# Third layer of a four-layer image kernel: powers taken from the unscaled symmetric matrix with a row scaling of each square, no transposition of the scaled matrix, and the last sum in token order

## Chip, cores and metric

The kernel runs on one core of one Trainium2 chip. The metric is the device time of one launch in microseconds (us). All tensors are float32 but for two small bfloat16 ones in the fourth layer.

## What is computed

The input is an image of 128 x 128 positions with 64 channels. Four layers follow one another, each as `x = x + layer(group_norm(x))`. The change is in the third layer alone. There, each of the 128 rows of the image is a graph of P = 128 nodes (tokens) with 64 features, and for every row the layer does this:

```python
def _build_A(pt, k):                       # k = 8
    x = pt - pt.mean(axis=-1, keepdims=True)
    x = x / (pt.std(axis=-1, ddof=1, keepdims=True) + 1e-06)
    corr = jnp.einsum('bnpd,bnqd->bnpq', x, x) / (D - 1 + 1e-06)
    ...                                    # mask: the 9 largest of each row of corr
    A = corr * mask
    A = 0.5 * (A + jnp.swapaxes(A, -1, -2))
    A = A + jnp.eye(P, dtype=A.dtype)
    deg = jnp.clip(A.sum(-1), 1e-06, None)
    dinv = deg ** (-0.5)
    return dinv[..., :, None] * A * dinv[..., None, :]
...
diff = alpha * (y - A y);  react = (A y) @ theta_w.T    # right side of an ODE, 8 Runge-Kutta steps of order 4
return relu(y_end)
```

The right side is linear in y, so eight steps are one polynomial of degree 32 in the matrix A = D^-1/2 M D^-1/2 (M symmetric 128 x 128, D its diagonal of degrees) and a 64 x 64 matrix that is the same for all rows. The kernel sums that polynomial in steps of A^4 and A^8 (Horner's rule).

## The kernel before, in words

The third layer is the function `layer2` (its name counts from 0), lines 1252 to 1667. It works on groups of ROWS = 4 rows, 32 groups. Every engine runs a loop of its own, written out by hand, over stages s = -1 to 33; in stage s the engines work on up to four groups at once, named by `stage(s)` (lines 1314 to 1317): `a` = s+1 (the next group is normed and transposed), `p` = s (the matrix M is prepared), `c` = s-1 (powers, and the first half of the polynomial), `r` = s-2 (the rest of the polynomial and the result). The order inside each loop is the order in which an engine issues; semaphores (`wait_ge`, `then_inc`) tie the engines together. PSUM, the memory that TensorE writes, has eight banks: B[0] squares, B[1] products with vectors, B[2] and B[3] (together `duo`) correlation, transpositions and the result, and four banks `quad`, one for each row of a group, which hold the running polynomial. SBUF tiles are slices of `nat` and `flat`.

One stage of TensorE, in its order, with the lines:

- L1574: transposes the normed tokens of `p`. L1528: `square(a1)`, which gives A^2 of `c`. L1540: one Horner step of `r` (two products of 128 x 128 by 128 x 128, accumulated in `quad`), after ACT has copied the last step's result out of `quad` (`keep_z`, L1362).
- L1547 and L1549, in `final(r, 0)`: the last sum. One transposition of the kept z for two rows, and two products whose stationary operand is z (64 columns) and whose moving operand is A^4, into the 64-partition halves of B[3], that is channel by token.
- L1591: sixteen instructions, y times A and y times A^2 for four rows. L1603: correlation of `p`. L1540, then L1528: A^4; L1611: transpositions; L1540; L1620: transposes the tokens of `a`.
- L1532: products with `theta`, 512 columns each, four calls, with `final(r, 1)`, L1637 and L1528 (A^8) between them. L1648: transposes the masked matrix of `p`. L1532: four more calls, and between them three Horner steps of `c` (L1540, `horner(c, 0, k)`) and L1662.
- L1662: transposes B = (scaled rows of M)/2 of `p` into B[3]; `b_ready` and `b_turned` stand around it. DVE then multiplies the rows of the transposed matrix with D^-1/2 again (L1516), which gives A (`a1`).

A call on a float32 operand is issued as two matmul instructions, a transposition as one.

The other engines, as far as they matter here:

- ACT copies every PSUM result that TensorE needs again: A^2 (L1389), A^4 (L1408), A^8 (L1422), the vectors (L1394, L1410, L1420), the correlation (L1399), the tokens (L1386, L1417), the Horner results (L1359, L1362), and takes two small square roots (L1425, L1428).
- DVE finishes a half group with three instructions (`finish`, L1439, L1442, L1444), finds the nine largest values of each row (L1455 to L1470), measures the next group (L1476, L1482), sums the degrees (L1487, L1491), takes reciprocals (L1496, L1501), scales rows (L1504), norms tokens (L1511), scales again (L1516) and sums the result for the next group norm (L1521, L1522).
- POOL adds the identity to the masked matrix (L1331), lays the finished group out for the fourth layer with four copies (L1343, L1344), and adds it into a sum (L1345). It does these in this order in each stage, and the copies wait for `x3_ready`.

## Time and profile before

| | us |
|---|---|
| three runs, median (lowest to highest) | 1161.11 (1156.29 to 1163.44) |
| the profiled execution, its own time | 1155.92 |
| its span, first to last instruction | 1154.1 |
| TensorE busy in the span | 1068.6 (93%) |
| VectorE (DVE) busy | 744.7 (65%) |
| ScalarE (ACT) busy | 522.6 (45%) |
| GpSimd (POOL) busy | 339.8 (29%) |

The profile is of one execution. PE is TensorE's matmuls, PEld its weight loads, which overlap them. A row of a timeline has the start, the duration from the first start to the last end of the instructions merged in it, the engine, the line, the operation, output and inputs by name with their shapes, and how many instructions are merged; in square brackets stands idle time just before, and what ended it. Matmuls are pipelined: the end of one overlaps the next, so what a block of them costs TensorE is the distance from its start to the start of the next block. A stage of the third layer recurs every 18.06 us; the stage looked at here begins at 706.56 us with L1574, and the next with the same instruction at 724.62.

### The profile page before, as it was taken

What the parts mean: (1) busy time and instruction counts of PE and PEld (TensorE: products, weight loads), DVE (VectorE), ACT (ScalarE), POOL (GpSimd) and SP (SyncE); (2) the same over time, 40 slices, a digit from 0 to 9 for tenths busy, and PEclk for the clock granted to TensorE, in tenths of its full rate; (3) what the DMA queues carried; (4) which work ended last, traced back from release to release, by engine and by line L of the source; (5) the groups of instructions that cost most, each with busy time, mean ns of one, the idle gap of its engine ahead of it and who ended that gap; (6) DMA issues with size and microseconds to landing.
All of it is one profiled execution on the core that took longest, in us unless ns stands there. A gap on an engine that the chain in (4) does not pass through costs nothing. (4 is left out here: it accounts for less than half of the span.)

```text
span 1154.1 us, 25407 instructions
## 1 busy us (share of the span) xinstructions
PE 1068.6 (93%) x9467; PEld 763.5 (66%) x9467; DVE 744.7 (65%) x3585; ACT 522.6 (45%) x1113; POOL 339.8 (29%) x476
## 2 busy tenths in 40 slices
PE   5887999999998799859999999999999999999788
PEld 3435888888886244437676776767777677776476
DVE  3675888888887332256767667676676766766245
ACT  2474777777776100134454444544445344453200
POOL 0142666666665100001212122121221212212211
PEclk8898999999999799869999999999999999999879
DMA  8000000000000000000000000000000000000012
GB/s 169 1 0 1 3 3 3 2 4 2 3 3 2 1 1 1 10 1 1 1 1 1 1 1 2 1 1 2 1 1 1 2 1 1 2 1 1 0 41 111
DMA packets 10461, 11.07 MB, mean 10 GB/s; under 512 B 3812, under 2 KB 8164, under 8 KB 10340
## 3 DMA queue, kind: packets, MB, share of 16 engines
q1 hardware_dynamic: 8964, 8.87, 2.9%
q8 instruction: 75, 1.23, 0.5%
q10 hardware_dynamic: 1376, 0.59, 0.3%
q14 instruction: 46, 0.38, 0.1%
HBM read 5.14 MB, written 4.23 MB: 8 GB/s over the span
## 5 line engine op out<-in xcount | busy, mean ns | idle before, releaser
L1532 PE MATMUL quad<-theta,nat 128*128 128x512 f32 x512 | 240.7, 593 | 0.0
L1331 POOL TENSOR_TENSOR nat<-nat,const 128x512 f32<-128x512 f32 x32 | 40.6, 1270 | 437.9 <-DVE nat L1470 437.9
L712 POOL TENSOR_TENSOR nat<-nat,arena 128x512 f32<-128x512 f32 x128 | 131.5, 1049 | 56.8 <-DVE arena L770 53.1
L1540 PEld LDWEIGHTS quad<-flat 128*128 128x128 f32 x768 | 104.9, 191 | 46.4 <-ACT flat L1362 25.0
L1532 PEld LDWEIGHTS quad<-theta,nat 128*128 128x128 f32 x512 | 87.5, 191 | 61.7 <-issue 61.7
L1540 PE MATMUL quad<-flat 128*128 128x128 f32 x768 | 124.1, 284 | 2.8 <-ACT flat L1362 1.7
L770 DVE CUSTOM_DVE_ANT_0 nat<-quad,arena 128x128 f32<-128x128 f32 x512 | 111.3, 283 | 2.0 <-PE quad L856 1.8
L1362 ACT ACTIVATE flat<-quad 128x256 f32<-128x256 f32 x192 | 73.3, 382 | 70.4 <-PE quad L1540 56.7
L729 ACT ACTIVATE nat<-bank 128x512 f32<-128x512 f32 x128 | 73.0, 597 | 65.8 <-PE bank L864 65.8
L1439 DVE SCALAR_TENSOR_TENSOR flat<-nat,c,duo 128x128 f32<-128x128 f32 x64 | 22.0, 344 | 102.6 <-PE duo L1549 102.6
L864 PE MATMUL bank<-const,nat 128*128 128x128 f32 x512 | 73.4, 276 | 8.0 <-ACT nat L729 8.0
L734 ACT ACTIVATE nat<-nat 128x512 f32<-128x512 f32 x128 | 77.2, 634 | 3.8 <-POOL nat L712 3.8
L1528 PE MATMUL bank<-nat 128*128 128x128 f32 x512 | 68.7, 278 | 0.3 <-DVE nat L1516 0.3
L864 PEld LDWEIGHTS bank<-const,nat 128*128 128x128 f32 x512 | 57.3, 141 | 15.9 <-ACT nat L729 15.6
L1528 PEld LDWEIGHTS bank<-nat 128*128 128x128 f32 x512 | 63.1, 194 | 0.8 <-DVE nat L1516 0.7
L1420 ACT ACTIVATE nat<-bank 128x512 f32<-128x512 f32 x32 | 19.1, 597 | 87.2 <-PE bank L1637 87.2
L1455 DVE MAX8 arena<-nat 128x8 f32<-128x128 f32 x128 | 27.9, 281 | 43.1 <-ACT nat L1399 43.1
L1487 DVE CUSTOM_DVE_ANT_0 nat<-nat,duo 128x128 f32<-128x128 f32 x128 | 29.2, 283 | 37.0 <-PE duo L1648 37.0
L770 DVE DVE_READ_ACCUMULATOR2_ANT arena<- 128x1 f32 x512 | 42.7, 83 | 0.0
L1344 POOL COPY img<-flat 64x256 f32<-64x256 f32 x64 | 39.6, 618 | 3.9
L1444 DVE SCALAR_TENSOR_TENSOR flat<-flat 128x128 f32<-128x128 f32 x64 | 38.3, 599 | 2.2
L840 PE MATMUL quad<-flat,w 64*128 64x256 f32 x256 | 37.2, 410 | 2.7 <-DVE arena L770 2.0
(393 smaller groups left out, 2236.7 us busy)
## 6 DMA issues: line engine op xcount, KB each, us to landing
out<-nat SPq DMA_DIRECT2D x16, 256.0 KB, 2.0
const<-in_constants ACTq DMA_DIRECT2D x1, 400.5 KB, 3.1
arena<-in_L_conv_Ws SPq DMA_DIRECT2D x1, 240.0 KB
flat<-arena SPq DMA_DIRECT2D x3, 32.0 KB, 4.4
nat<-in_x SPq DMA_DIRECT2D x4, 0.2 KB, 11.6
arena<-in_L_conv_Wq ACTq DMA_DIRECT2D x1, 32.0 KB, 6.2
arena<-in_L_conv_Wk ACTq DMA_DIRECT2D x1, 32.0 KB, 5.3
arena<-in_L_conv_Wv ACTq DMA_DIRECT2D x1, 32.0 KB, 5.0
```

The costliest lines, as they stand in the source:

```text
L712: pool.tensor_tensor(scored, scored, of_head(least[b], h).broadcast_to([128, ROWS, L]), ALU.subtract).then_inc(lowered, 1)
L729: act.activation(pT[r], m.bank[r % 2][:, :], ACT.Copy).then_inc(kept, 1)
L734: act.activation(t, t, ACT.Exp, scale=-1.0).then_inc(exps_done, 1)
L770: last = dve.tensor_tensor_reduce(prob[b][:, at(r, h)], m.quad[:, h, row(r)], m.bias[:, row(h)], -1.0, BIG, ALU.add, ALU.min, least[b][:, ...
L864: last = pe.transpose(m.bank[r % 2][:, row(h)], prob[g % 2][:, at(r, h)], ident)
L1331: pool.tensor_tensor(quarters(rem), quarters(rem), ident.unsqueeze(1).broadcast_to([128, ROWS, 128]), ALU.add).then_inc(diag_added, 1)
L1344: step(pool.tensor_copy(m.cols3[:, :, ROWS * r + e:ROWS * (r + 1):2].rearrange("p j t -> p t j"), source))
L1362: act.activation(kept, m.quad[:, HALF * half:HALF * (half + 1), place * C:(place + 2) * C], ACT.Copy).then_inc(z_ready[half], 1)
L1444: dve.scalar_tensor_tensor(out=x_of(g, half), in0=held[half], scalar=0.0, in1=x_of(g, half), op0=ALU.max, op1=ALU.add).then_inc(x3_ready[h ...
L1528: last = pe.matmul(B[0][:, col(n)], source[:, col(n)], source[:, col(n)], start=True, stop=True)
L1532: return pe.matmul(m.quad[:, n, :], vT[:, col(n)], m.theta[:, part, :], start=(part == 0), stop=False, skip_group_check=True)
L1540: last = pe.matmul(m.quad[:, row, place * C:(place + 2) * C], a8[g % 2][:, col(row)], zs[half][k % 2][:, n, :], start=False, stop=(k == 2) ...
```

## The change

The unscaled matrix M is used in place of A, with S = D^-1: the kernel keeps A1 = S M, and squares as (S M)^T times M = M S M. A square is then the symmetric "plain" matrix (`h2`, `h4`), and multiplying its rows with S gives the "scaled" one (`a2`, `a4`, `a8`). So:

- The transposition L1662 and the product L1516 behind it are gone, as are `b_ready` and `b_turned`. DVE makes `a1` with one scaling of the summed matrix (new L1530).
- A^2 and A^4 are copied out of PSUM by ACT (`h2`, new L1397; `h4`, new L1417) and then scaled, A^2 by DVE (new L1473, both inputs in SBUF) and A^4 by POOL (new L1331). A^8 is scaled by DVE straight out of PSUM (new L1513), and ACT's copy L1422 is gone.
- The tokens enter scaled by D^1/2, by POOL in place (new L1341, `yn_weighed`), and the result is scaled back with D^-1/2 by DVE (`weigh`, new L1451).
- The last sum is made in token order: `sum_up` (new L1579) has A^4 as the stationary operand (128 columns), 64 moving columns, and accumulates into `quad`; after `weigh`, two transpositions (new L1675) bring the group to channel order in B[3], and DVE finishes the whole group at once with two instructions (`finish`, new L1458, L1461), now near the end of its stage.
- On TensorE the correlation (L1603, now L1621) stands ahead of the products with A and A^2 (L1591, now L1630). ACT's order of the two copies (L1394, L1399) is as before.

TensorE, steady state, in the kernel before, at the end of a stage: the first two Horner steps of group `c`, with the transposition of B between them:

```order
L1540 MATMUL quad<-flat 128x128 [waits l2_z_ready_first,l2_a8_ready]
L1540 MATMUL quad<-flat 128x128
L1662 MATMUL duo<-const,nat 128x128 [waits l2_held_ready_last,l2_b_ready]
L1662 MATMUL duo<-const,nat 128x128 x3
L1540 MATMUL quad<-flat 128x128 [waits l2_z_ready_first]
```

The same place on TensorE in the changed kernel, up to the first instructions of the next stage:

```order
L1570 MATMUL quad<-flat 128x128 [waits l2_z_ready_first,l2_a8_ready]
L1570 MATMUL quad<-flat 128x128
L1570 MATMUL quad<-flat 128x128 [waits l2_z_ready_first]
L1570 MATMUL quad<-flat 128x128
L1562 MATMUL quad<-theta,nat 128x512
L1570 MATMUL quad<-flat 128x128 [waits l2_z_ready_first]
```

Between the two Horner steps nothing stands now. TensorE in the kernel before, at the start of a stage (turn of the normed tokens, `square`, Horner step, `final`, the products with A and A^2, the correlation):

```order
L1574 MATMUL duo<-const,nat 128x128 [waits l2_xs_ready]
L1574 MATMUL duo<-const,nat 128x128
L1528 MATMUL bank<-nat 128x128 [waits l2_a8_ready,l2_a1_ready]
L1528 MATMUL bank<-nat 128x128 x3
L1540 MATMUL quad<-flat 128x128 [waits l2_z_ready_last]
L1540 MATMUL quad<-flat 128x128
L1547 MATMUL duo<-const,flat 128x128 [waits l2_z_ready_first,l2_held_ready_last]
L1549 MATMUL duo<-flat 64x128 x2
L1591 MATMUL bank<-nat 64x128 [waits l2_v34_ready,l2_a2_ready]
L1591 MATMUL bank<-nat 64x128 x7
L1603 MATMUL duo<-nat 128x128 [waits l2_a1_ready,l2_held_ready_first,l2_xsT_ready]
L1603 MATMUL duo<-nat 128x128 x3
```

And the same place on TensorE in the changed kernel:

```order
L1604 MATMUL duo<-const,nat 128x128 [waits l2_xs_ready]
L1604 MATMUL duo<-const,nat 128x128
L1558 MATMUL bank<-nat 128x128 [waits l2_a8_ready,l2_a1_ready]
L1558 MATMUL bank<-nat 128x128 x3
L1570 MATMUL quad<-flat 128x128 [waits l2_z_ready_last]
L1570 MATMUL quad<-flat 128x128
L1579 MATMUL quad<-flat 128x64 [waits l2_z_ready_first]
L1579 MATMUL quad<-flat 128x64
L1621 MATMUL duo<-nat 128x128 [waits l2_held_ready,l2_xsT_ready]
L1621 MATMUL duo<-nat 128x128 x3
L1630 MATMUL bank<-nat 64x128 [waits l2_v34_ready,l2_a2_ready,l2_yn_weighed]
L1630 MATMUL bank<-nat 64x128 x7
```

`final`'s three calls became two with 64 moving columns, and the correlation moved ahead of the products that wait for `a2_ready`.

DVE in the kernel before, across the end of a stage: the norm of the tokens, the second scaling, the sums of the finished group, and then `finish` of the next group's first half ahead of the search:

```order
L1511 TENSOR_SCALAR nat<-nat,arena 128x64 x3
L1516 TENSOR_TENSOR nat<-duo,arena 128x512 [waits l2_b_turned]
L1521 BN_STATS stats<-flat 128x6 [waits l2_x3_ready_last,l2_x3_ready_first]
L1522 TENSOR_REDUCE rowsum<-flat 128x2
L1439 SCALAR_TENSOR_TENSOR flat<-nat,c,duo 128x128 [waits l2_final_made_first]
L1442 TENSOR_TENSOR flat<-flat,duo 128x128 [waits l2_held_ready_first]
L1444 SCALAR_TENSOR_TENSOR flat<-flat 128x128 [waits l2_held_ready_first]
L1455 MAX arena<-nat 128x8 [waits l2_cor_ready]
```

The same place on DVE in the changed kernel: `finish` of a whole group, its sums, then the scaling of A^2 and `weigh`:

```order
L1545 TENSOR_SCALAR nat<-nat,arena 128x64 x3
L1458 SCALAR_TENSOR_TENSOR flat<-nat,c,duo 128x256 [waits l2_final_made]
L1461 SCALAR_TENSOR_TENSOR flat<-flat 128x256 [waits l2_held_ready]
L1551 BN_STATS stats<-flat 128x6 [waits l2_x3_ready]
L1552 TENSOR_REDUCE rowsum<-flat 128x2
L1473 TENSOR_TENSOR nat<-nat,arena 128x512 [waits l2_v34_made,l2_h2_ready]
L1451 TENSOR_TENSOR flat<-quad,arena 128x128 [waits l2_final_made,l2_summed]
L1480 MAX arena<-nat 128x8 [waits l2_cor_ready]
```

In the kernel before, `finish` of the second half (again L1439, L1442, L1444) stood right behind the search (L1470), so the instruction that releases POOL's copies has moved from the middle of the stage to its end. POOL's order in a stage was L1331 (identity), copies, L1345; it is now the product for A^4 (new L1331), the identity (new L1337), the product on the tokens (new L1341), copies, sum. The core of the diff:

```diff
@@ gpsimd
+                if c is not None:
+                    pool.wait_ge(h4_ready, c + 1)
...
+                    pool.tensor_tensor(quarters(a4[c % 2]), quarters(h4), square_inv.unsqueeze(2).broadcast_to([128, ROWS, L]),
+                                       ALU.mult).then_inc(a4_ready, 1)
...
+                    pool.wait_ge(dsq_ready, p + 1)
+                    fresh = quarters(yn[p % 2])
+                    pool.tensor_tensor(fresh, fresh, dsq.unsqueeze(2).broadcast_to([128, ROWS, C]), ALU.mult).then_inc(yn_weighed, 1)
@@ scalar
-                    act.activation(a2, B[0][:, :], ACT.Copy).then_inc(a2_ready, 1)
+                    act.activation(h2, B[0][:, :], ACT.Copy, scale=0.5).then_inc(h2_ready, 1)
...
-                    act.activation(a4[c % 2], B[0][:, :], ACT.Copy).then_inc(a4_ready, 1)
+                    act.activation(h4, B[0][:, :], ACT.Copy).then_inc(h4_ready, 1)
...
-                    act.wait_ge(a8_made, c + 1)
-                    act.activation(a8[c % 2], B[0][:, :], ACT.Copy).then_inc(a8_ready, 1)
@@ vector
+            def weigh(g, half):
+                dve.wait_ge(summed, 2 * g + half + 1)
...
+                dve.tensor_tensor(weighed[half].rearrange("p (n x) -> p n x", n=HALF), m.quad[:, HALF * half:HALF * (half + 1), 0:C],
+                                  dinv[g % 4][:, HALF * half:HALF * (half + 1)].unsqueeze(2).broadcast_to([128, HALF, C]),
+                                  ALU.mult).then_inc(weighed_ready, 1)
+            def finish(g):
+                dve.wait_ge(final_made, g + 1)
+                dve.scalar_tensor_tensor(out=held, in0=yT[g % 4], scalar=m.c0[:, :], in1=B[3][:, 0:PAIR],
+                                         op0=ALU.mult, op1=ALU.add).then_inc(held_ready, 1)
+                dve.wait_ge(held_ready, g + 1)
+                dve.scalar_tensor_tensor(out=x_of(g), in0=held, scalar=0.0, in1=x_of(g),
+                                         op0=ALU.max, op1=ALU.add).then_inc(x3_ready, 1)
...
+                if c is not None:
+                    dve.wait_ge(h2_ready, c + 1)
...
+                    dve.tensor_tensor(quarters(a2), quarters(h2), by_degree(square_inv), ALU.mult).then_inc(a2_ready, 1)
...
+                    dve.tensor_tensor(quarters(a8[c % 2]), quarters(B[0][:, :]), by_degree(square_inv), ALU.mult).then_inc(a8_ready, 1)
...
-                    dve.wait_ge(b_turned, p + 1)
-                    dve.tensor_tensor(quarters(a1), quarters(B[3][:, :]), dinv.unsqueeze(2).broadcast_to([128, ROWS, L]),
-                                      ALU.mult).then_inc(a1_ready, 1)
                 if r is not None:
+                    finish(r)
@@ tensor
-            def square(source):
+            def square(scaled, plain):
                 for n in range(ROWS):
-                    last = pe.matmul(B[0][:, col(n)], source[:, col(n)], source[:, col(n)], start=True, stop=True)
+                    last = pe.matmul(B[0][:, col(n)], scaled[:, col(n)], plain[:, col(n)], start=True, stop=True)
...
-                pe.transpose(B[3][:, L:2 * L], zs[half][1][:, 0, :], ident)
-                for e in range(HALF):
-                    last = pe.matmul(B[3][e * C:(e + 1) * C, 0:L], zs[half][1][:, 1, e * C:(e + 1) * C], a4[g % 2][:, col(HALF * half + e)],
-                                     start=True, stop=True, skip_group_check=True)
+                for n in range(HALF):
+                    row = HALF * half + n
+                    last = pe.matmul(m.quad[:, row, 0:C], a4[g % 2][:, col(row)], zs[half][1][:, n, 0:C],
+                                     start=False, stop=True, skip_group_check=True)
+                last.then_inc(summed, 1)
...
+                    for half in range(2):
+                        last = pe.transpose(B[3][:, col(half)], weighed[half], ident)
+                    last.then_inc(final_made, 1)
...
-                    pe.wait_ge(b_ready, p + 1)
...
-                    for n in range(ROWS):
-                        last = pe.transpose(B[3][:, col(n)], cor[:, col(n)], ident)
-                    last.then_inc(b_turned, 1)
```

## Rows read from the trace of the kernel before

**Rows 1.** Busy time of the engines, third layer; the last columns are granted clock, DMA share, GB/s

```profile
525.00:1067.00 542.00, 540.97 (x3661) 389.76 (x3660) 375.01 (x1876) 247.29 (x598) 120.69 (x180) 1.00 0.01 1
```

**Rows 2.** Timeline of TensorE's matmuls, end of one stage and the next

```profile
703.62 0.61 PE L1540 MATMUL quad<-flat 128*128 128x128 f32 x4
704.10 0.66 PE L1662 MATMUL duo<-const,nat 128*128 128x128 f32 x4
704.71 0.71 PE L1540 MATMUL quad<-flat 128*128 128x128 f32 x4
...
706.56 0.38 PE L1574 MATMUL duo<-const,nat 128*128 128x128 f32 x2
706.78 1.06 PE L1528 MATMUL bank<-nat 128*128 128x128 f32 x8
707.67 0.61 PE L1540 MATMUL quad<-flat 128*128 128x128 f32 x4
708.12 0.27 PE L1547 MATMUL duo<-const,flat 128*128 128x128 f32 x1
...
708.59 1.04 PE L1591 MATMUL bank<-nat 128*64 128x128 f32 x16
709.58 0.71 PE L1603 MATMUL duo<-nat 64*128 64x128 f32 x8
710.22 0.71 PE L1540 MATMUL quad<-flat 128*128 128x128 f32 x4
...
714.49 0.27 PE L1547 MATMUL duo<-const,flat 128*128 128x128 f32 x1
...
715.06 1.16 PE L1637 MATMUL bank<-nat 128*128 128x128 f32 x8
...
718.66 0.60 PE L1648 MATMUL duo<-const,nat 128*128 128x128 f32 x4
```

**Rows 3.** Timeline of TensorE's matmuls, last stages of the layer

```profile
1081.13 0.61 PE L1540 MATMUL quad<-flat 128*128 128x128 f32 x4
1082.21 0.71 PE L1540 MATMUL quad<-flat 128*128 128x128 f32 x4 [0.47 <-ACT flat L1362]
```

**Rows 4.** Timeline of TensorE in the second layer, and clock of that stretch (columns as in rows 1)

```profile
415.81 1.94 PE L1232 MATMUL quad<-const,arena 1*128 1x1 f32 x16
417.69 0.64 PE L1169 MATMUL quad<-img,arena 64*64 64x512 f32 x1
...
415.50:417.70 2.20, 2.20 (x20) 1.87 (x19) 0.00 (x0) 0.00 (x0) 0.00 (x0) 1.00 0.00 0
```

**Rows 5.** Timeline of ACT in the same stage as rows 2

```profile
707.87 0.60 ACT L1389 ACTIVATE nat<-bank 128x512 f32<-128x512 f32 x1 [0.18 <-PE bank L1528]
...
709.68 0.60 ACT L1394 ACTIVATE nat<-bank 128x512 f32<-128x512 f32 x1 [0.94 <-PE bank L1591]
710.33 0.60 ACT L1399 ACTIVATE nat<-duo 128x512 f32<-128x512 f32 x1
```

**Rows 6.** Timeline of DVE in that stage

```profile
709.51 0.29 DVE L1444 SCALAR_TENSOR_TENSOR flat<-flat 128x128 f32<-128x128 f32 x1
710.96 0.87 DVE L1455 MAX8 arena<-nat 128x8 f32<-128x128 f32 x4 [1.16 <-ACT nat L1399]
...
715.00 0.69 DVE L1470 SCALAR_TENSOR_TENSOR nat<-nat 128x512 f32<-128x512 f32 x1
715.61 0.34 DVE L1439 SCALAR_TENSOR_TENSOR flat<-nat,c,duo 128x128 f32<-128x128 f32 x1
...
716.31 0.95 DVE L1444 SCALAR_TENSOR_TENSOR flat<-flat 128x128 f32<-128x128 f32 x1
...
719.30 0.29 DVE L1487 CUSTOM_DVE_ANT_0 nat<-nat,duo 128x128 f32<-128x128 f32 x1 [1.11 <-PE duo L1648]
...
720.26 0.21 DVE L1491 TENSOR_SCALAR arena<-arena 128x4 f32<-128x4 f32 x1
...
720.95 0.88 DVE L1504 TENSOR_SCALAR nat<-nat,arena 128x128 f32<-128x128 f32 x4
721.74 0.98 DVE L1511 TENSOR_SCALAR nat<-nat,arena 128x64 f32<-128x64 f32 x4
```

**Rows 7.** Timeline of POOL in that stage

```profile
715.84 1.27 POOL L1331 TENSOR_TENSOR nat<-nat,const 128x512 f32<-128x512 f32 x1 [13.18 <-DVE nat L1470]
717.42 0.39 POOL L1343 COPY img<-flat 64x256 f32<-64x256 f32 x1 [0.30 <-DVE flat L1444]
...
719.71 0.73 POOL L1345 TENSOR_TENSOR arena<-arena,flat 128x256 f32<-128x256 f32 x1
```

More of the change, by code:

```diff
@@ L1275, in layer2 @@
     yn = [t[:, k:k + PAIR] for t in (next(nat_tiles),) for k in (0, PAIR)]
-    cor, rem, a1, a2, v12T, v12n, v34T = (next(nat_tiles) for _ in range(7))
+    cor, rem, a1, h2, a2, h4, v12T, v12n, v34T = (next(nat_tiles) for _ in range(9))
     a4, a8 = ([next(flat_tiles) for _ in range(2)] for _ in range(2))
     zs = [[t[:, k:k + PAIR].rearrange("p (n x) -> p n x", n=HALF) for t in (next(flat_tiles),) for k in (0, PAIR)] for _ in range(2)]
-    held = [t[:, 0:L] for t in (next(flat_tiles), next(flat_tiles))]
+    held = next(flat_tiles)[:, 0:PAIR]
+    weighed = [t[:, k:k + L] for t in (next(flat_tiles),) for k in (0, L)]
     st = m.take(6 * ROWS)
     mv = m.take(2 * ROWS).rearrange("p (r s) -> p r s", s=2)
-    std, rstd, deg, dsq, dinv = (m.take(ROWS) for _ in range(5))
+    std, rstd, deg, dsq, square_inv = (m.take(ROWS) for _ in range(5))
+    dinv = [m.take(ROWS) for _ in range(4)]
     top = m.take(8 * ROWS)
@@ L1471, in _ @@
                 if r is not None:
-                    finish(r, 1)
+                    weigh(r, 1)
                 if a is not None:
@@ L1491, in _ @@
                     dve.tensor_scalar(deg, deg, 0.5, 1e-6, ALU.mult, ALU.max).then_inc(deg_ready, 1)
+                    dve.wait_ge(deg_ready, p + 1)
+                    if p > 0:
+                        dve.wait_ge(a4_ready, p)
+                    dve.reciprocal(square_inv, deg).then_inc(square_inv_ready, 1)
+                    dve.wait_ge(square_inv_ready, 2 * p + 1)
+                    if p > 0:
+                        dve.wait_ge(a2_made, p)
+                    for n in range(ROWS):
+                        last = dve.tensor_scalar(a1[:, col(n)], cor[:, col(n)], square_inv[:, n:n + 1], 0.5, ALU.mult, ALU.mult)
+                    last.then_inc(a1_ready, 1)
                 if a is not None:
@@ L1498, in _ @@
                     dve.wait_ge(dsq_ready, p + 1)
[L1499 to L1505 removed]
+                    dve.reciprocal(dinv[p % 4], dsq).then_inc(square_inv_ready, 1)
                 if a is not None:
@@ L1542, in horner, with sum_up @@
                 last.then_inc(horner_made[half], 1)
[L1544 removed]
+            def sum_up(g, half):
                 pe.wait_ge(z_ready[half], 4 * g + 4)
[L1547 to L1551 removed]
+                for n in range(HALF):
[3 more added lines that the diff above has]
+                last.then_inc(summed, 1)
             def kind_weights():
@@ L1579, in _ @@
                         pe.wait_ge(a8_ready, c)
-                    square(a1).then_inc(a2_made, 1)
+                    square(a1, cor).then_inc(a2_made, 1)
                 if r is not None:
                     horner(r, 1, 0)
-                    pe.wait_ge(held_ready[1], 2 * r)
-                    final(r, 0)
+                    sum_up(r, 0)
+                if p is not None:
+                    pe.wait_ge(xsT_ready, p + 1)
+                    if r is not None and r > 0:
+                        pe.wait_ge(held_ready, r)
+                    for t in range(HALF):
+                        for e in range(2):
+                            half = xsT[e * C:(e + 1) * C, col(t)]
+                            last = pe.matmul(B[2 + e][:, col(t)], half, half, start=True, stop=True)
+                    last.then_inc(cor_made, 1)
                 if c is not None:
+                    pe.wait_ge(yn_weighed, c + 1)
                     pe.wait_ge(a2_ready, c + 1)
@@ L1593, in _ @@
                     last.then_inc(v12_made, 1)
-                if p is not None:
-                    pe.wait_ge(xsT_ready, p + 1)
-                    if r is not None:
-                        pe.wait_ge(held_ready[0], 2 * r + 2)
-                    if c is not None:
-                        pe.wait_ge(a1_ready, c + 1)
-                    for t in range(HALF):
-                        for e in range(2):
-                            half = xsT[e * C:(e + 1) * C, col(t)]
-                            last = pe.matmul(B[2 + e][:, col(t)], half, half, start=True, stop=True)
-                    last.then_inc(cor_made, 1)
                 if r is not None:
@@ L1629, in _ @@
                 if r is not None:
-                    if p is not None:
-                        pe.wait_ge(cor_ready, p + 1)
-                    pe.wait_ge(held_ready[0], 2 * r + 2)
-                    final(r, 1)
+                    sum_up(r, 1)
                 if c is not None:
@@ L1656, in _ @@
                     horner(c, 0, 0)
-                if p is not None:
-                    pe.wait_ge(b_ready, p + 1)
-                    if r is not None:
-                        pe.wait_ge(held_ready[1], 2 * r + 2)
-                    for n in range(ROWS):
-                        last = pe.transpose(B[3][:, col(n)], cor[:, col(n)], ident)
-                    last.then_inc(b_turned, 1)
                 if c is not None:
```

88 lines of the change are left out of this document (44 added, 44 removed).

## The prediction

> **What bounds the kernel now.** I read busy time by stretch first, then TensorE's timeline over one stage, then those of ACT, DVE and POOL at the same times. In the third layer TensorE is busy 540.97 of 542.00 us at a granted clock of 1.00, its level of 2.4 GHz, and DVE, ACT and POOL 375, 247 and 121 us [rows 1]. So the layer costs what TensorE's stage costs, 18.06 us, unless another engine makes TensorE wait. In rows 2 the reader is to take distances between starts: 706.56 to 706.78 is 0.22 us for two transpositions, 706.78 to 707.67 is 0.89 for eight instructions of 128 columns, 0.111 each. "Busy" hides one thing: from 704.10 to 704.71 TensorE spends 0.61 on four transpositions (L1662) that take 0.44 at 0.111 each; it is waiting there.
>
> **The change part by part.** All offsets are from the start of a stage, 706.56.
>
> *L1662 goes, and returns nothing.* It stands between the Horner steps that start at 703.62 and 704.71, 1.09 apart [rows 2]. The second needs ACT's copy of the first's result. In the drain, where no L1662 stands between them, the same two start at 1081.13 and 1082.21, 1.08 apart, the second released by ACT L1362 [rows 3]. The transpositions lay inside that wait. What is late next is the copy itself, as before: gain 0.01, taken as 0.
>
> *The last sum.* `final` takes 0.47 (708.12 to 708.59) and 0.57 (714.49 to 715.06), 1.04 together [rows 2]. In its place come two calls of `sum_up` for each half, eight instructions in a stage, and two transpositions, 0.22 as L1574. No row has 64 moving columns behind a load of 128 at the full clock. From below: if moving columns set the pace, half of 0.111, 0.055. From above: sixteen instructions with one moving column and 128 loaded take 415.81 to 417.69, 0.117 each, at a clock of 1.00 [rows 4]. That row is nearer, since narrowing to one column did not make them faster than 128 columns: the load sets the pace. I take 0.11: 0.88 + 0.22 - 1.04 = +0.06 us a stage. With 0.055 it is 0.44 + 0.22 - 1.04 = -0.38. The Trainium skill ("TensorE: Matmul & The Clock Gate", section "Back-to-back issue gap") has about 60 cycles for a matmul of up to 64 columns, 0.025 us at 2.4 GHz; by it the sum would be 0.20 + 0.22 - 1.04 = -0.62. Its section on LDWEIGHTS has the number of loaded columns over 1.2 in ns, 107 ns here, which agrees with the 0.117 of rows 4 and not with its other figure.
>
> *The scaled A^2, a longer path into the sixteen instructions (L1630).* The square starts at +0.22; ACT began its copy at +1.31 and took 0.60 [rows 5], so `h2` is there at +1.91. DVE, idle then, starts the new product at +1.94. It is of L1470's kind and shape (two SBUF inputs, 128 x 512): 0.69 [rows 6], so `a2` would be there at +2.63 and L1630 start at +2.68. TensorE's cover, with the correlation (709.58 to 710.22, 0.64) moved ahead, is 0.22 + 0.89 + 0.45 + 0.44 + 0.64 = 2.64. Undisturbed, the wait is 0.04.
>
> *But POOL is at work then.* DVE's second L1444 takes 0.95 from 716.31, against 0.29 at 709.51 [rows 6]; both its inputs are in SBUF. POOL's L1331 runs from 715.84 to 717.11 [rows 7], and L1444 ends at 717.26: it stood until POOL was done, and ended 0.15 later. In the kernel before, POOL idles when a stage begins. Now its copies wait for `x3_ready` from the end of DVE's stage. Working that out: from L1648 to the next stage's start is 724.62 - 718.66 = 5.96, all TensorE's and unchanged. DVE starts the degree sums 0.64 after L1648 and L1491 0.96 later [rows 6]; then the reciprocal (0.20) and its result (0.21), four scalings 0.79 (720.95 to 721.74), three small ones 0.58, L1545 0.98, `finish` 0.48 and 0.43 (0.34 and 0.29 for 128 columns, and 0.13 for 128 more, which is what 512 against 128 columns cost L1470: 0.40 for 384), and 0.07 for two hand-overs: 0.64 + 0.96 + 0.41 + 0.79 + 0.58 + 0.98 + 0.98 = 5.34. POOL starts 0.16 after such an end (717.26 to 717.42), at 5.50, thus 0.46 before the stage ends. Its five instructions take 3.02 (717.42 to 720.44) [rows 7], so the last, L1353, runs from about +1.8 to +2.5. DVE's product comes at +1.94, in the midst of it, and stands until about +2.5 (from my steps, +2.48 to +2.56; I take 2.48). It then ends 0.15 + 0.40 later, at +3.03, and L1630 starts at +3.05: wait 0.41. Behind L1630 everything on TensorE shifts by it. Bounds: 0.04 where the product meets a gap, 0.6 where it meets L1353's start (0.73 to stand).
>
> *What is hidden.* ACT's correlation copy still stands behind its copy of L1630's result, so the search starts later: in the kernel before at +4.40 (710.96), now at 3.05 + 0.99 + 0.10 + 0.65 + 0.63 = +5.42 [rows 2, 5, 6]. `weigh` of the second half starts 4.65 later (710.96 to 715.61), takes about 0.29, and is there at +10.4. The theta product that waits for it stands 0.64 and 0.13 nearer to L1630 than before: 715.06 - 708.59 = 6.47, less 0.77, is 5.70, and 16 instructions of 0.111 are 1.8, so it comes at 3.05 + 7.5 = +10.55. So 0.15 of slack, the thinnest one. POOL's identity ends about +11.6, L1682 comes at +12.6. POOL's new product for A^4, 1.27 as L1331, ends about +7.6, the square that needs it comes at +9.75. ACT loses a copy of 0.60, DVE gets 0.69 for A^8 inside its wait for L1648 (1.11 idle in rows 6), and POOL's product on the tokens ends a stage ahead of its use. All these cost nothing; without that cover `weigh` would cost what it is late.
>
> *Sum.* L1630 starts at +3.05 instead of 2.03 + 0.64 = 2.67 with the correlation counted: +0.38. The second half: 0.44 + 0.22 - 0.57 = +0.09. Together +0.47 a stage, over 30 stages +14.1. At the ends: one stage without a correlation has 0.5 less cover; the last group has one more hop between DVE and TensorE, about 0.6; the first search starts some 0.4 later behind ACT. With +1.5 for these the sum is +15.6. Against the profiled execution's own 1155.92 (a span of 1154.1 and 1.8 around it) that is 1171.5. That execution lies 5.2 below the median of the three runs, so I put the sum on the mean of all four times, 1159.2: 1174.8.
>
> **The rivals.**
>
> *No clash on the port.* If POOL's phase is 0.3 later than I worked out, DVE's product slips in before L1353, or if 0.5 earlier, behind it. For it: my chain of 12 steps decides about 0.25 us. Against it: POOL is at work for 3.0 us around that time, and most shifts only change which instruction DVE meets. Per stage 0.04 + 0.09 = 0.13: 3.9 + 1.5, 1164.6. Chance 0.27.
>
> *Narrow matmuls at half price.* With the clash, L1630's start is fixed by `a2`, so only the second half gains: 0.38 + 0.22 + 0.22 - 0.57 = +0.25 a stage, 1168.2; without the clash -0.09 a stage, 1158. Rows 4 speak against. Chance 0.07.
>
> *Faster: L1662's time comes back.* If the second Horner step at 704.71 waited for L1662's own delay (it shares the queue with `b_ready`) and not for ACT's copy, 0.61 a stage goes: 0.47 - 0.61 = -0.14, 1156.5 with the clash, and -0.48 a stage, 1146.3, without. It decides from the point where two Horner steps can start less than 1.08 apart; rows 3 show they can't. With other gains that I don't see, chance 0.09.
>
> *The search is slowed by POOL.* POOL's product for A^4 runs from about +6.3 to +7.6, in the midst of DVE's search. If it blocked the search for up to 1.27, `weigh` would be up to 1.0 late for theta: up to 30 us more, 1195 for two thirds of that. No row has POOL and this search at one time. The search's instructions have one SBUF tensor each, unlike L1444. Chance 0.07. The Trainium skill ("SBUF — State Buffer", section "Who interferes with whom") says that a DVE instruction with at most one SBUF input, outside certain modes, does not contend with GpSimd; by it this rival costs nothing and the clash on A^2 stands.
>
> **How the numbers follow.** Forecast 0.50, no clash 0.27, half price 0.07, faster 0.09, slowed search 0.07. A measurement here can tell about 1% (11.6 us) from no change. The forecast's own range is 1168 to 1180 (a wait of 0.2 to 0.6). Slower by over 1% is above 1170.8: most of the forecast and the slowed search, 0.48. Within 1%: no clash, half price, the weak end of the forecast, half of the faster case: 0.44. Faster by over 1%: 0.08. The range runs from 1157 (the faster case with the clash) to 1184 (a full wait, put on the median of 1161.1).
>
> **What would show it.** Right: L1570 to L1570 at the end of a stage still 1.08 apart, now with idle time between; eight L1579 at 0.11 each; L1473 taking 1.1 instead of 0.69 and ending 0.15 + 0.40 after POOL's L1353; TensorE waiting about 0.4 before L1630 for DVE L1473; a stage of 18.5 us. Wrong: L1473 at 0.69 (no clash), L1579 at 0.06, Horner steps closer than 1.08, or waits of theta (L1562) for DVE L1451.

## The result, and the profile after

The changed kernel takes 1178.49 us (median of four runs, 1175.56 to 1180.79) against 1161.33 for the kernel before, measured beside it (four runs, 1156.29 to 1163.44). The ratio is 1.0156, its 95% interval 1.0124 to 1.0188: slower by 1.6%. The forecast was 1174.8, within 1157 to 1184. The profiled execution took 1175.56 with a span of 1173.7, so +19.6 in both against before. Offsets below count from a stage's start, the first transposition of normed tokens (L1574 before, L1604 after).

First the third layer by windows, the row that answers to [rows 1]: window and length, then busy us (and instructions) of TensorE, its loads, DVE, ACT and POOL, TensorE's clock, DMA share and GB/s.

```profile
525.00:1067.00 542.00, 514.38 (x3429) 383.54 (x3430) 376.45 (x1830) 211.71 (x553) 165.69 (x227) 1.00 0.00 1
```

At the same clock TensorE now idles 27.6 of 542 us, where it idled 1.0. ACT has lost 36 us of work, POOL gained 45. The view of waits, for TensorE from 540 to 1085, says before which line the idle time stands, and what ended it (us in all, times, longest):

```profile
PE quad L1570 <- ACT flat L1368: 14.2, 30, 0.5
PE bank L1630 <- issue: 14.0, 26, 0.5
```

Two waits share it. The first is the one in which L1662 used to stand and which cost time before, too. The second is new. It has no releaser in this view, so the lines that it could wait for have to be read. TensorE's timeline over one stage, 713.17 to 731.88, for [rows 2]:

```profile
710.24 0.61 PE L1570 MATMUL quad<-flat 128*128 128x128 f32 x4
711.32 0.71 PE L1570 MATMUL quad<-flat 128*128 128x128 f32 x4 [0.47 <-ACT flat L1368]
...
713.17 0.38 PE L1604 MATMUL duo<-const,nat 128*128 128x128 f32 x2
713.39 1.06 PE L1558 MATMUL bank<-nat 128*128 128x128 f32 x8
...
714.73 0.56 PE L1579 MATMUL quad<-flat 128*128 128x64 f32 x4
715.22 0.71 PE L1621 MATMUL duo<-nat 64*128 64x128 f32 x8
716.48 1.09 PE L1630 MATMUL bank<-nat 128*64 128x128 f32 x16 [0.54 <-issue]
...
723.99 1.88 PE L1562 MATMUL quad<-theta,nat 128*128 128x512 f32 x4
...
731.88 0.38 PE L1604 MATMUL duo<-const,nat 128*128 128x128 f32 x2
```

A stage takes 18.71 where it took 18.06. L1630 starts at +3.31. TensorE was free at 715.94 (its row less the 0.54 of idle time), at +2.77. DVE and POOL at the same time, for [rows 6] and [rows 7]:

```profile
715.12 1.26 DVE L1473 TENSOR_TENSOR nat<-nat,arena 128x512 f32<-128x512 f32 x1 [1.71 <-ACT nat L1397]
...
723.39 0.28 DVE L1451 TENSOR_TENSOR flat<-quad,arena 128x128 f32<-128x128 f32 x1
...
727.94 1.23 DVE L1530 TENSOR_SCALAR nat<-nat,arena 128x128 f32<-128x128 f32 x4
...
730.90 0.42 DVE L1461 SCALAR_TENSOR_TENSOR flat<-flat 128x256 f32<-128x256 f32 x1
```

```profile
715.10 0.72 POOL L1353 TENSOR_TENSOR arena<-arena,flat 128x256 f32<-128x256 f32 x1
719.82 1.04 POOL L1331 TENSOR_TENSOR flat<-nat,arena 128x512 f32<-128x512 f32 x1 [3.99 <-ACT nat L1417]
728.01 0.69 POOL L1341 TENSOR_TENSOR nat<-nat,arena 128x256 f32<-128x256 f32 x1 [3.13 <-ACT arena L1438]
731.49 0.39 POOL L1351 COPY img<-flat 64x256 f32<-64x256 f32 x1 [2.79 <-DVE flat L1461]
```

DVE's product is ready to start at +1.95, 0.02 after POOL's L1353 has started. POOL is done at 715.82, DVE at 716.38, 0.56 later, and TensorE starts at 716.48. So DVE stood until POOL was done, and then worked 0.56.

The profile also holds stages without the clash. In the one that starts at 695.03 DVE was the first, by 0.09:

```profile
695.03 0.38 PE L1604 MATMUL duo<-const,nat 128*128 128x128 f32 x2
...
697.77 1.09 PE L1630 MATMUL bank<-nat 128*64 128x128 f32 x16
```

```profile
696.98 0.69 DVE L1473 TENSOR_TENSOR nat<-nat,arena 128x512 f32<-128x512 f32 x1 [1.58 <-ACT nat L1397]
```

```profile
697.07 1.18 POOL L1353 TENSOR_TENSOR arena<-arena,flat 128x256 f32<-128x256 f32 x1
```

Here DVE took 0.69, POOL was the one that was held (1.18 instead of 0.72), L1630 came at +2.74 and the stage (to 713.17) took 18.14. The next stage fell into the clash. Another of these stages, which starts at 825.38, shows which of POOL's instructions matters:

```profile
827.32 0.69 DVE L1473 TENSOR_TENSOR nat<-nat,arena 128x512 f32<-128x512 f32 x1 [1.49 <-ACT nat L1397]
```

```profile
826.81 0.62 POOL L1352 COPY img<-flat 64x256 f32<-64x256 f32 x1
```

DVE started while POOL's copy still had 0.11 to go, and took its 0.69 all the same. So the copy did not hold it, where the sum, L1353, does.

Over the layer the 29 stages from 527.28 to 1067.40 take 540.1, where the same 29 took 523.6 before (526.02 to 1049.59): +16.5 of the 19.6. The rest is at the two ends: the first of these stages starts 1.3 later, the end of the layer is 1.0 longer (up to the first matmul behind it, at 1095.68 before and 1114.48 after), and 0.8 come behind that.

### The profile page after: what moved, and what is told of

Read it like the earlier page. It is cut to its first block and busy times, and to the rows that moved or that the text cites. A ratio compares the mean times of both kernels' runs of the same rounds, so it can differ in the third digit from the quotient of the medians.

```text
span 1173.7 us, 25304 instructions
## 1 busy us (share of the span) xinstructions
PE 1059.5 (90%) x9339; PEld 771.6 (66%) x9339; DVE 758.5 (65%) x3585; ACT 491.9 (42%) x1081; POOL 397.2 (34%) x540
## 5 line engine op out<-in xcount | busy, mean ns | idle before, releaser
L1562 PE MATMUL quad<-theta,nat 128*128 128x512 f32 x512 | 240.9, 593 | 0.0
L1562 PEld LDWEIGHTS quad<-theta,nat 128*128 128x128 f32 x512 | 87.4, 191 | 61.2 <-issue 61.2
L1331 POOL TENSOR_TENSOR flat<-nat,arena 128x512 f32<-128x512 f32 x32 | 33.3, 1041 | 135.6 <-ACT nat L1417 135.6
L1337 POOL TENSOR_TENSOR nat<-nat,const 128x512 f32<-128x512 f32 x32 | 40.6, 1269 | 102.6 <-DVE nat L1495 102.6
L1473 DVE TENSOR_TENSOR nat<-nat,arena 128x512 f32<-128x512 f32 x32 | 36.8, 1149 | 58.3 <-ACT nat L1397 58.3
L1351 POOL COPY img<-flat 64x256 f32<-64x256 f32 x64 | 25.4, 397 | 99.3 <-DVE flat L1461 97.3
L1341 POOL TENSOR_TENSOR nat<-nat,arena 128x256 f32<-128x256 f32 x32 | 21.8, 682 | 98.7 <-ACT arena L1438 98.7
L1630 PE MATMUL bank<-nat 128*64 128x128 f32 x512 | 35.9, 282 | 14.9 <-issue 14.6
```

The costliest lines, as they stand in the source:

```text
L1337: pool.tensor_tensor(quarters(rem), quarters(rem), ident.unsqueeze(1).broadcast_to([128, ROWS, 128]), ALU.add).then_inc(diag_added, 1)
L1473: dve.tensor_tensor(quarters(a2), quarters(h2), by_degree(square_inv), ALU.mult).then_inc(a2_ready, 1)
L1562: return pe.matmul(m.quad[:, n, :], vT[:, col(n)], m.theta[:, part, :], start=(part == 0), stop=False, skip_group_check=True)
L1630: last = pe.matmul(B[1][e * C:(e + 1) * C, col(n)], yn[c % 2][:, col(n, C)], power[:, col(n)], start=True, stop=True, skip_group_check=True)
```

## The experiments

The theory: L1473 stands behind POOL's L1353, 0.56 a stage, and nearly all of the loss is that. The rivals: TensorE's own order and the new last sum cost it; or the missing L1662 plays a part. Each ratio below is against the kernel before, run beside it.

**POOL's copies moved out of the way.** They and the sum (put together as `lay`) go behind the product for A^4, a stage later:

```diff
+                if r is not None and r > 0:
+                    if c is not None:
+                        pool.wait_ge(a4_ready, c + 1)
+                    lay(r - 1)
```

> The changed kernel, but POOL lays a group out and adds it to the sum one stage later, behind its product for A^4, so that it is idle when DVE scales A^2. Theory (port clash): DVE's L1473 takes 0.69 us instead of 1.26, TensorE stops waiting ahead of the products with A and A^2 (L1630), the stage goes from 18.70 to about 18.2 us, and the time from 1178 to about 1163. Rival (the wait is the extra hop over DVE itself, not the clash): L1473 shorter or not, stage and time stay within 3 us of the changed kernel.

Measured: 1162.63, ratio 1.0029 (1.0013 to 1.0044). TensorE's timeline, then DVE's:

```profile
710.07 0.38 PE L1606 MATMUL duo<-const,nat 128*128 128x128 f32 x2
...
728.21 0.38 PE L1606 MATMUL duo<-const,nat 128*128 128x128 f32 x2
```

```profile
712.01 0.69 DVE L1475 TENSOR_TENSOR nat<-nat,arena 128x512 f32<-128x512 f32 x1 [1.70 <-ACT nat L1399]
```

The product starts at +1.94, as in the changed kernel, takes 0.69, and the stage 18.14. All work is still there, only its time differs. The clash alone is 18.70 - 18.14 = 0.56 a stage. In the new place one of POOL's copies meets the last instruction of the search (L1497 here, two SBUF inputs, 128 x 512) with 0.37 to go, and that instruction takes 0.75 instead of 0.69: 0.06 beside a copy, against 0.57 beside the sum.

**The product read from PSUM.** DVE scales A^2 straight from TensorE's result; ACT's copy and the next square are ordered behind it.

```diff
-                    dve.wait_ge(h2_ready, c + 1)
+                    dve.wait_ge(a2_made, c + 1)
...
-                    dve.tensor_tensor(quarters(a2), quarters(h2), by_degree(square_inv), ALU.mult).then_inc(a2_ready, 1)
+                    dve.scalar_tensor_tensor(out=quarters(a2), in0=quarters(B[0][:, :]), scalar=0.5, in1=by_degree(square_inv),
+                                             op0=ALU.mult, op1=ALU.mult).then_inc(a2_ready, 1)
```

> The changed kernel, but DVE makes the scaled A^2 straight out of PSUM (one SBUF input), ahead of ACT's copy h2. Theory: an instruction with one SBUF input isn't held up by POOL, so it takes 0.69 us although POOL's copies run, a2 is there 1.2 us earlier, no wait ahead of the products with A and A^2, stage about 18.2 us, time about 1163. Rival (any DVE work beside POOL's is slowed): L1473's successor still takes 1.1 to 1.3 us; the time still falls, by less, since it starts 0.6 us earlier.

Measured: 1161.68, ratio 1.0022 (1.0007 to 1.0038), a stage of 18.09 (709.10 to 727.19). DVE:

```profile
710.41 0.69 DVE L1474 SCALAR_TENSOR_TENSOR nat<-bank,arena 128x512 f32<-128x512 f32 x1 [1.08 <-PE bank L1560]
```

In this stage it is mostly a copy that POOL works on beside it (L1352, 710.31 to 710.94), which would not have held the old product either. One stage, at the end of the layer, has the sum at work before DVE starts:

```profile
1071.89 0.69 DVE L1474 SCALAR_TENSOR_TENSOR nat<-bank,arena 128x512 f32<-128x512 f32 x1 [2.11 <-PE bank L1560]
```

```profile
1071.47 0.72 POOL L1353 TENSOR_TENSOR arena<-arena,flat 128x256 f32<-128x256 f32 x1
```

POOL's sum had 0.30 to go, and DVE took 0.69, where the product from SBUF, meeting the last 0.34 of the same sum, takes 0.89 (next experiment). The Trainium skill ("SBUF — State Buffer", section "Who interferes with whom") exempts DVE instructions with at most one SBUF input, outside certain modes; here the inputs are PSUM and a small SBUF one, and the trace agrees. The product is also ready 1.2 earlier, so the time of this run alone does not part the port from the hop over ACT; the experiment before it does.

**A shorter product on the tokens.** Only the first of 64 channels is scaled, the others are left unscaled, to see what sets POOL's phase:

```diff
-                    pool.tensor_tensor(fresh, fresh, dsq.unsqueeze(2).broadcast_to([128, ROWS, C]), ALU.mult).then_inc(yn_weighed, 1)
+                    pool.tensor_tensor(fresh[:, :, 0:1], fresh[:, :, 0:1], dsq.unsqueeze(2), ALU.mult).then_inc(yn_weighed, 1)
```

> The changed kernel with POOL's product on the tokens cut from 256 to 4 columns; the rest of the tokens stays unscaled, so that work is left out. Theory (phase of POOL's work): DVE's four scalings L1530 take 0.88 us instead of 1.23, DVE finishes the group 0.35 us earlier, POOL's sum ends 0.35 us earlier, L1473 takes about 0.9 instead of 1.26 us, stage about 18.35, time about 1168. Rival (L1473's length doesn't depend on POOL's phase): the same 18.70 and 1178.

Measured: 1168.79, ratio 1.0091 (1.0061 to 1.0121), a stage of 18.33 (715.67 to 734.00). DVE:

```profile
730.06 0.88 DVE L1530 TENSOR_SCALAR nat<-nat,arena 128x128 f32<-128x128 f32 x4
...
735.94 0.89 DVE L1473 TENSOR_TENSOR nat<-nat,arena 128x512 f32<-128x512 f32 x1 [2.07 <-ACT nat L1397]
```

```profile
735.56 0.72 POOL L1353 TENSOR_TENSOR arena<-arena,flat 128x256 f32<-128x256 f32 x1
```

The four scalings take 0.88 instead of 1.23, so 0.35 of L1530 in the changed kernel was POOL's L1341 beside it, which holds DVE's scaling though that has one tensor input. All that follows on DVE and POOL comes earlier, POOL's L1353 at +1.56 instead of +1.93, and DVE meets only its last 0.34 (735.94 to 736.28). The loss per stage falls with it, from 0.65 to 0.28. That is the dose that the theory wants.

**Work put back into L1662's place.** Four transpositions of a constant between the first two Horner steps, with no wait of their own:

```diff
+                    for n in range(ROWS):
+                        pe.transpose(B[0][:, col(n)], ident, ident)
```

> The changed kernel with four transpositions of a constant put back between the first two Horner steps of a stage, where L1662 stood. Theory (they lay inside the wait for ACT's copy): 0 us, the two Horner steps stay 1.08 apart, time within 3 us of the changed kernel's. Rival (removing L1662 did give its time back, and something else ate it): plus 0.44 to 0.61 us a stage, 13 to 18 us, about 1194.

Measured: 1178.6, ratio 1.0164 (1.0129 to 1.0199), a stage of 18.70. TensorE:

```profile
732.29 0.61 PE L1570 MATMUL quad<-flat 128*128 128x128 f32 x4
732.74 0.60 PE L1692 MATMUL bank<-const 128*128 128x128 f32 x4
733.37 0.71 PE L1570 MATMUL quad<-flat 128*128 128x128 f32 x4
```

The steps are 1.08 apart with four instructions between them, as without. The deleted work was worth nothing there.

**Twice the columns in the last sum**, on top of the PSUM product. The added 64 columns go to an unused part of the same bank.

```diff
-                    last = pe.matmul(m.quad[:, row, 0:C], a4[g % 2][:, col(row)], zs[half][1][:, n, 0:C],
+                    last = pe.matmul(m.quad[:, row, 0:2 * C], a4[g % 2][:, col(row)], zs[half][1][:, n, 0:2 * C],
```

> e2_psum with 128 moving columns instead of 64 in the last sum (the other 64 are not used; work is added). Theory (the load of 128 stationary columns sets the pace): still 0.11 us an instruction, stage and time as e2_psum within 3 us. Rival (moving columns set it): plus 8 x 0.055 = 0.44 us a stage, about 13 us.

Measured: 1161.24, ratio 1.0029 (1.0009 to 1.0050), a stage of 18.15, +0.06 against 18.09.

```profile
715.06 0.61 PE L1581 MATMUL quad<-flat 128*128 128x128 f32 x4
715.60 0.71 PE L1623 MATMUL duo<-nat 64*128 64x128 f32 x8
```

The block takes 0.54 with 128 columns and 0.49 with 64 (714.73 to 715.22 above). That of the other half takes 0.44 and 0.39, but there the block behind it (L1662 in the changed kernel) is 0.05 longer after the narrow one. Halving the moving columns gives back 0.05 us a stage, not the 0.44 that half of eight instructions would be.

**The turn of the result put into the gap**, on top of the PSUM product: the two transpositions behind `weigh` go between the first two Horner steps.

```diff
-                if r is not None:
-                    pe.wait_ge(weighed_ready, 2 * r + 2)
...
-                    last.then_inc(final_made, 1)
...
                     horner(c, 0, 0)
+                if r is not None:
+                    pe.wait_ge(weighed_ready, 2 * r + 2)
...
+                    for half in range(2):
+                        last = pe.transpose(B[3][:, col(half)], weighed[half], ident)
+                    last.then_inc(final_made, 1)
```

> e2_psum with the two transpositions of the result moved into the wait between the first two Horner steps. Theory (0.64 us of TensorE stand empty there in each stage): minus 0.22 us a stage, about 7 us below e2_psum, near 1156, that is a little below the kernel before. Rival (no room there, or DVE's later finish holds the next stage up): as e2_psum or above.

Measured: 1153.22, ratio 0.9961 (0.9941 to 0.9980): faster than before. A stage takes 17.875, 0.22 less than with the PSUM product alone.

```profile
724.02 0.61 PE L1572 MATMUL quad<-flat 128*128 128x128 f32 x4
724.47 0.38 PE L1692 MATMUL duo<-const,flat 128*128 128x128 f32 x2
725.10 0.71 PE L1572 MATMUL quad<-flat 128*128 128x128 f32 x4 [0.26 <-ACT flat L1368]
```

The pair costs its 0.22 where it stood, and nothing between these two. This is what removing L1662 was worth: an empty place to put work into.

**The correlation put back behind the products**, once alone and once on the PSUM product.

```diff
-                if p is not None:
-                    pe.wait_ge(xsT_ready, p + 1)
...
-                    last.then_inc(cor_made, 1)
                 if c is not None:
...
+                if p is not None:
+                    pe.wait_ge(xsT_ready, p + 1)
...
+                    last.then_inc(cor_made, 1)
```

> The changed kernel with the correlation behind the products with A and A^2 again, as in the kernel before. Theory (the correlation covers the wait for a2): the products still start 3.3 us into the stage, the correlation's 0.64 us comes on top, stage about 19.3, time about 1197. Rival (the new order itself costs, or is neutral): time at or below the changed kernel's 1178.

Measured: 1200.13, ratio 1.0357 (1.0338 to 1.0376), a stage of 19.34:

```profile
724.59 0.38 PE L1604 MATMUL duo<-const,nat 128*128 128x128 f32 x2
...
727.88 1.09 PE L1621 MATMUL bank<-nat 128*64 128x128 f32 x16 [1.17 <-issue]
```

The products start at +3.29 (727.88), as they did with the correlation ahead (+3.31): their start is set by DVE, not by TensorE. Only the wait is longer, 1.17 against 0.54, by the cover taken away.

> e2_psum with the correlation behind the products again. Theory: a2 is there at 2.15 us into the stage, TensorE at 2.05, so the order hardly matters: stage within 0.1 us and time within 4 us of e2_psum. Rival (cover is needed even then): plus 0.4 us a stage or more, over 12 us.

Measured: 1163.2, ratio 1.0033 (1.0014 to 1.0052), a stage of 18.15:

```profile
729.75 0.38 PE L1606 MATMUL duo<-const,nat 128*128 128x128 f32 x2
...
731.86 1.09 PE L1623 MATMUL bank<-nat 128*64 128x128 f32 x16
```

With the product ready early, they start at +2.11, and the order matters little (18.15 against 18.09).

**The gap filled to the brim.** On top of the turn in the gap, the first 128 columns of two theta products (of rows 2 and 3 of the group) are split off and put there as well.

```diff
-            def theta(n, vT, part):
+            def theta(n, vT, part, first=0, end=512):
...
-                    theta(2, v34T, 1)
+                    theta(2, v34T, 1, L)
                     horner(c, 0, 0)
...
+                    theta(2, v34T, 1, 0, L)
+                    theta(3, v34T, 1, 0, L)
                     horner(c, 0, 1)
-                    theta(3, v34T, 1)
+                    theta(3, v34T, 1, L)
```

> e6_turn_in_gap with 0.42 us more of TensorE's own work in the wait between the first two Horner steps: the first 128 of 512 columns of the two theta products on each side of it, issued there. Theory (0.64 us of the gap stand empty, e6 has filled 0.22): minus 0.42 us a stage, 12 to 13 us below e6, about 1141. Rival (the products moved were themselves covering the copies that the first and the third Horner step wait for, so the wait comes back there): within 3 us of e6_turn_in_gap.

Measured: 1152.25, ratio 0.9930 (0.9904 to 0.9957), where about 1141 was expected: a miss, and by the time within the range of the rival reading. A stage takes 17.70, 0.175 less than with the turn alone, where 0.42 was expected.

```profile
701.46 0.68 PE L1573 MATMUL quad<-flat 128*128 128x128 f32 x4
701.98 0.38 PE L1693 MATMUL duo<-const,flat 128*128 128x128 f32 x2
702.19 0.61 PE L1564 MATMUL quad<-theta,nat 128*128 128x128 f32 x4
702.64 0.68 PE L1573 MATMUL quad<-flat 128*128 128x128 f32 x4
703.16 0.81 PE L1564 MATMUL quad<-theta,nat 128*128 128x384 f32 x2
703.81 0.70 PE L1573 MATMUL quad<-flat 128*128 128x128 f32 x4
```

The gap is full: the two Horner steps are now 1.18 apart instead of 1.08, and that is TensorE's own work (0.52 + 0.22 + 0.45) without idle time. Part of what the gap took in came back elsewhere, and ACT's rows show how. This is its copy ahead of the third Horner step:

```profile
703.36 0.38 ACT L1368 ACTIVATE flat<-quad 128x256 f32<-128x256 f32 x1 [0.80 <-PE quad L1573]
```

It ends at 703.74, 0.06 before the step at 703.81. The copies for the first and the second step end 0.14 and 0.08 before them. With the turn alone the three distances are 0.28, 0.05 and 0.28. The three steps, to the start of what follows, take 0.52, 0.52 and 0.54 here, and 0.45, 0.55 and 0.45 there. So in both runs a step whose copy ended 0.14 or less before it takes 0.52 to 0.55, and one with 0.28 to spare 0.45. The theta pieces that were moved had been covering the copies for the first and the third step, as the rival reading of this run had it. No run isolates this, so it is a reading of the rows. The stage adds up: 0.33 less in the two theta blocks around the gap (0.42 less 0.09, by which the first step starts late), 0.10 more in the gap, 0.09 more in the third step, 0.03 less in the second.

**The same in the kernel before**: one theta piece of 128 columns behind L1662.

```diff
-                    theta(2, v34T, 1)
+                    theta(2, v34T, 1, L)
...
+                    theta(2, v34T, 1, 0, L)
```

> The kernel before with one such quarter of a theta product behind L1662. Theory: 0.17 us are left empty beside the four transpositions there, so minus 0.17 us a stage, 5 us, about 1155: the room that the change opens (0.44 us more) is what e9 has over this. Rival (the gap before wasn't empty by 0.17): within 2 us of the kernel before.

Measured: 1162.6, ratio 1.0014 (0.9995 to 1.0034), where about 1155 was expected: a miss. The stage takes 18.00 against 18.05 (the 29 stages of the kernel before took 523.6), so 0.05 less where 0.17 was expected, and the time shows none of it.

```profile
721.50 0.68 PE L1541 MATMUL quad<-flat 128*128 128x128 f32 x4
722.02 0.60 PE L1663 MATMUL duo<-const,nat 128*128 128x128 f32 x4
722.46 0.39 PE L1532 MATMUL quad<-theta,nat 128*128 128x128 f32 x2
722.68 0.69 PE L1541 MATMUL quad<-flat 128*128 128x128 f32 x4
```

It is the same as in the run before: the first step takes 0.52 and not 0.45, since ACT's copy now ends 0.14 before it, and with 0.52 + 0.44 + 0.22 the two steps are 1.18 apart instead of 1.08. (One stage of the 29, at 703.45, took 18.06; there the transpositions start only at 704.05, 0.06 after DVE's last scaling L1504, so they waited for `b_ready`, which that instruction gives.) The gap of the kernel before had hardly room for two more instructions. The change takes four out of it, and that makes the room.

## Why the prediction was right, and what it mis-sized

**L1662 returns nothing.** Right. The two Horner steps are 1.08 apart as forecast, with 0.47 idle between them, and refilling the gap moved nothing (1178.6 against 1178.49).

**The last sum.** Right: the four instructions with 128 loaded and 64 moving columns take 0.49 up to the next block in the first half and 0.39 in the second, together 0.88, 0.11 each as taken, and not half of it. With 0.22 for the turn (725.71 to 725.93) that is the forecast's +0.06 against 1.04. The block behind the second half's sum takes 0.95 where it took 0.99 (L1662, before L1637), so behind L1630 the stage takes 15.40 against 18.06 - 2.67 = 15.39 before: +0.01 there where +0.09 was forecast, +0.03 over the whole stage. The price of about 60 cycles for a matmul of up to 64 columns, in the Trainium skill ("TensorE: Matmul & The Clock Gate", section "Back-to-back issue gap"), would have given about 0.1 for these four by an estimate; the page gives it for a matmul by itself, with no load counted, and the trace does not agree with it behind a load of 128 float32 columns.

**The clash.** Right in kind, in place and in sign. DVE's product started at +1.95 (forecast +1.94), POOL's L1353 was then at work, DVE ended 0.56 after POOL (forecast 0.55), and TensorE followed in 0.10 (forecast 0.02). L1630 came at +3.31 where I had +3.05. Of the 0.26, 0.17 is the end of L1353, at +2.65: out of my own +2.48 to +2.56 I had taken the lower, which is 0.08 of it, POOL started 0.07 later than forecast, and its five instructions took 3.04 and not 3.02. 0.08 is the hand-over, 0.01 DVE's 0.56.

The step that failed is "four scalings 0.79" in the chain of DVE's end of stage. I took it from L1504, which is the same kind of instruction from SBUF to SBUF, and did not ask what POOL does beside it in the changed kernel. It does the new product on the tokens (L1341, 728.01 to 728.70), and one of the four is held by it: they take 1.15 up to the next instruction (727.94 to 729.09). The short-product run has a row of 0.88 for the four, the changed kernel 1.23. Other terms of that chain were too long: three small ones 0.41 and not 0.58, L1545 0.89 and not 0.98 (I had taken its duration, not the distance between starts), `finish` with its hand-overs 0.94 and not 0.98. So of the 0.36 only 0.07 arrived at POOL's start (0.39 before the stage's end, forecast 0.46).

That was luck, and the forecast hung on it. With that one term right and the others as I had them, POOL would have started 0.10 before the stage's end and L1353 at about +2.2, behind DVE's product at +1.94: no clash, by my own rival. I had also counted POOL as at work for 3.0 us around that time, whatever the shift; but four of its five instructions are copies, and the stage at 825.38, in which POOL was 0.2 late, had its product beside a copy at full speed. Only L1353, 0.7 long, can meet it.

The wait is 0.54 and not 0.41 + 0.26, because the cover was 2.77 where I had 2.64: the last sum and the correlation (0.49 and 0.72) are each a little longer.

**The sum.** +0.65 a stage instead of +0.47; the clash is 0.56 of it by the first experiment. The 29 stages that can be compared would make +18.8; four of them escaped the clash (three because DVE was first, and the first stage, in which POOL has no copies yet), which leaves the +16.5 read above. The ends are +3.1 where +1.5 was taken. Together +19.6 on the profiled execution, forecast +15.6; in the medians +17.2.

**What was said to be hidden** was hidden. POOL's product for A^4 (719.82 to 720.86) ran in the midst of the search, which took the 4.66 from 718.73 to `weigh` at 723.39 that it took before (4.65): that rival is excluded by this row. (The prediction gave each instruction of the search one SBUF tensor; the last one, L1495 from 722.78, has two, but POOL was done 1.9 before it.) `weigh` ended at 723.67, and theta (L1562) started at 723.99: 0.32 of slack, forecast 0.15.

**The rival "no clash"**, at 1164.6, is what two experiments made by hand, at 1162.6 and 1161.7. Its mechanism occurs in the kernel itself, in three stages. With 0.27 it had too little: L1353 starts only 0.02 us ahead of DVE's product, and without the luck above, by these numbers, the rival would have come true.

**Beyond the prediction.** I judged the change by what it removed and saw an emptied place as worthless. Filled with the two transpositions and without the clash, the kernel takes 1153.22, with two theta pieces besides 1152.25: 0.4% and 0.7% faster than before, and the two best of those run. The forecast for the second was 11 us too low.

## What to carry to other kernels

- When a change moves the instruction that releases POOL, lay POOL's phase, its arithmetic on two tensors above all, over the DVE instructions with two SBUF inputs, the new ones, and over those of the tail that sets that phase. A product that TensorE waits for is better read from PSUM, if its source is there.
- An instruction that lies inside a wait is worth nothing when deleted, but the wait is then a place: move independent work of the same engine into it, and check first what that work covers where it stands now. The theta pieces had covered two other waits, and 0.42 us of them returned 0.175.
- With float32 and 128 loaded columns, count instructions, not moving columns: half the columns in the same eight instructions bought 0.05 us a stage.

## What was not expected of the hardware

- A hair's breadth decides 0.56 us a stage. With POOL's L1353 0.02 ahead, DVE's L1473 takes 1.26 and POOL 0.72; with DVE 0.09 ahead, DVE takes 0.69 and POOL 1.18. Whichever is first runs at its own speed and the other stands. That is between DVE's product and POOL's sum; POOL's copies did not do it (0.69 beside one, and 0.75 for the search's last instruction in the first experiment).
- A scaling of a float32 tile by one value per partition, from SBUF to SBUF, is held by POOL as well, though it has a single tensor input. The row of L1530 (lowest, median and highest ns, then the stretch):

```profile
L1530 DVE TENSOR_SCALAR nat<-nat,arena x128: 272/276/640, 505.5 to 1083.0; 128x128 f32<-128x128 f32 x128
```

  The Trainium skill ("SBUF — State Buffer", section "Who interferes with whom") names such modes of tensor_scalar; the 0.640 beside the median of 0.276 agrees, and the short-product run took the delay away.
- The round trip of a Horner step over ACT was 1.08 with a gap empty, with two or with four transpositions in it, and 1.18 when it held six instructions, in both kernels. Of the 0.10, 0.07 is the first step's own four instructions, which take 0.52 instead of 0.45 when ACT's copy ends only 0.14 ahead of them.
